# Reordering ScalarE's and VectorE's work in the attention head groups of a fused decoder block

## The reference, cut to what matters

```python
x = x + attn(layernorm(x))      # 16 heads of 32, ALiBi bias, 30*tanh(s/30), causal softmax
x = x + xattn(layernorm(x), memory, mask)     # one head, width 512, 128 memory rows
x = x + ffn(layernorm(x))       # silu(x @ q(gate_w) * sg) * (x @ q(up_w) * su) @ q(down_w) * sd
```

## Time and profile before

| | |
|---|---|
| time, median of 3 runs (lowest to highest) | 563.09 us (561.78 to 563.39) |
| time of the profiled execution | 563.1 us |
| its span, first to last instruction | 561.0 us |
| mean granted TensorE clock | 0.994 of full |
| TensorE busy | 547.0 us, 97% of the span |
| VectorE, ScalarE, GpSimd busy | 352.7, 268.0, 286.4 us |
| transposes of group 2 (head group 2 of g = 1) | begin at 114.06 us |
| `scores(2, 0)` | begins at 132.44 us |
| `scores` on TensorE | 1.4 us, `context` 1.9 us, a projection of 12 products 2.8 us |
| four transposes of one tile on TensorE | 0.37 us from one tile to the next |
| `normalize_context` on VectorE | 2.6 us (112.41 to 115.05) |
| GpSimd rounds a slab behind `low_part` of head group 2 | 117.37 to 120.23, 193.02 to 195.67, 260.61 to 263.26 |
| attention ends, feed-forward begins | about 262.7 us |

### The profile page before, as it was taken

One profiled execution on the slowest core, in us unless ns is written; L12 is line 12 of the kernel. 1 busy time (PEld: TensorE's weight loads), 2 busy tenths in 40 slices (PEclk: granted clock), 3 DMA queues, 4 the chain that ended last, 5 costly groups with the idle time before them and its releaser, 6 DMA issues.

```text
span 561.0 us, 10139 instructions
## 1 busy us (share of the span) xinstructions
PE 547.0 (97%) x3946; PEld 428.9 (76%) x3946; DVE 352.7 (63%) x701; ACT 268.0 (48%) x485; POOL 286.4 (51%) x258
## 2 busy tenths in 40 slices
PE   8999999989989999999999999999999999999997
PEld 7787888768868888888888888766686667866675
DVE  7997877895676667578787885345633564244422
ACT  6747976856845687567744352033401333023310
POOL 4297798965494554996794336324400343013320
PEclk9999999989989999999999999999999999999999
DMA  8951231452123520129571902200001000100001
GB/s 295 339 212 39 78 96 56 150 190 77 39 77 94 171 56 3 58 69 285 204 270 55 302 3 92 77 0 1 1 37 39 0 1 0 58 19 1 0 20 56
DMA packets 43422, 50.74 MB, mean 90 GB/s; under 512 B 2544, under 2 KB 25072, under 8 KB 43376
## 3 DMA queue, kind: packets, MB, share of 16 engines
q1 hardware_dynamic: 43376, 50.10, 27.2%
HBM read 36.46 MB, written 13.63 MB: 89 GB/s over the span
## 4 chain that ended last, share of the span: by engine, by line
PE 83%; POOL 7%; DVE 5%; ACT 2%; issue 2%; DMA 1%; DVEq 0%; ACTq 0%; POOLq 0%
PE bank L287 34%; PE bank L433 23%; PE bank L453 16%; PE bank L282 2%; PE bank L375 2%; PE bank L360 2%; POOL x_res L735 2%; PE bank L385 2%; POOL q_w L721 2%; POOL q_w L719 2%; POOL probs L712 1%; DVE q_m L1200 1%; PE bank L352 1%; POOL reduced L704 1%; ACT kT L856 1%
## 5 line engine op out<-in xcount | busy, mean ns | idle before, releaser
L287 PE MATMUL bank<-reduced 128*128 128x512 f32 x936 | 226.0, 398 | 3.5 <-DVE x_res L1167 2.6
L287 PEld LDWEIGHTS bank<-reduced 128*128 128x128 f32 x936 | 175.2, 190 | 42.2 <-issue 4.9
L814 POOL TENSOR_TENSOR f_parts<-fused,f_parts 128x512 fp32r<-128x512 f32 x48 | 62.9, 1310 | 159.3 <-ACT f_parts L1047 159.3
L1029 ACT ACTIVATE tanh_g<-bank,half_gate 128x512 f32<-128x512 f32 x48 | 33.0, 688 | 150.8 <-PE bank L433 139.2
L453 PE MATMUL bank<-reduced,f_parts 128*128 128x512 f32 x384 | 88.4, 390 | 0.0
L453 PEld LDWEIGHTS bank<-reduced,f_parts 128*128 128x128 f32 x384 | 71.8, 188 | 15.0
L1361 DVE SCALAR_TENSOR_TENSOR silu<-tanh_g,bank 128x512 f32<-128x512 f32 x48 | 32.9, 685 | 64.0 <-ACT tanh_g L1029 63.9
L433 PE MATMUL bank<-reduced 128*128 128x512 f32 x288 | 72.0, 402 | 0.0
L433 PEld LDWEIGHTS bank<-reduced 128*128 128x128 f32 x288 | 54.1, 188 | 12.9
L712 POOL TENSOR_SCALAR_AFFINE_SELECT probs<-probs 128x1024 f32<-128x1024 f32 x32 | 36.9, 1160 | 44.9 <-ACT probs L881 44.9
L719 POOL TENSOR_TENSOR q_w<-q_w,q_m 128x512 f32<-128x512 f32 x36 | 49.3, 1370 | 10.2 <-DVE q_m L1202 10.2
(11 more groups left out here) (123 smaller groups left out, 725.8 us busy)
## 6 DMA issues: line engine op xcount, KB each, us to landing
quantized<-q_w SPq DMA_DIRECT2D x36, 256.0 KB, 3.3
reduced<-quantized SPq DMA_DIRECT2D x12, 512.0 KB, 7.0
memT_sb<-in_memT SPq DMA_DIRECT2D x16, 256.0 KB, 5.0
mem_sb<-in_mem SPq DMA_DIRECT2D x16, 256.0 KB, 5.6
out<-y_sb SPq DMA_DIRECT2D x16, 256.0 KB, 2.0
q_w<-in_gate_w SPq DMA_DIRECT2D x12, 256.0 KB, 3.1
q_w<-in_up_w SPq DMA_DIRECT2D x12, 256.0 KB, 3.2
x_res<-in_x SPq DMA_DIRECT2D x3, 1024.0 KB, 9.3
```

Source lines behind the costliest of these rows:

```text
L287: ins = pe.matmul(dst, stationary, moving, start=(n == 0), stop=(n == len(pairs) - 1))
L814: pool.tensor_tensor(f_lo[:, f, :], fused[:, f % 2, :], f_hi[:, f, :].bitcast(F32), ALU.subtract).then_inc(f_lo_ready, 1)
L1029: act.activation(tanh_g[:, f % 2, :], src[:], ACT.Tanh, scale=half_gate[:, f:f + 1]).then_inc(tanh_ready, 1)
```

## The change

No instruction is added or removed. The order in three queues and two bank numbers change:

- TensorE: `turn_x(g + 1, 2)` writes the bank of Q and `turn_x(g + 1, 3)` that of K; before it was the other way round.
- ScalarE, head group 0 of g = 2 and 3: the second exponential of the probabilities is taken ahead of `cross_second(g - 2, 3)` and `cross_first(g - 2, 4)`.
- ScalarE, head group 2: Q is copied out ahead of K, and the high part of the context is made between the second and third turned tile, not ahead of all four.
- VectorE, head group 1, g of 1 and more: the third tile of the output projection is added ahead of the third slab's preparation.
- VectorE, head group 2, g of 1 and more: of the four normalized tiles for cross attention only the first is made ahead of the low parts of the turned tiles, three behind them.
- VectorE, head group 3: of the next group's statistics one tile stands ahead of cross attention's step 1 and three, with the moments, behind it.

```diff
@@ TensorE, head group 2
                 for i in range(GT):
-                    turn_x(g + 1, i, (S_BANK, S_BANK + 1, K_BANK, Q_BANK)[i])
+                    turn_x(g + 1, i, (S_BANK, S_BANK + 1, Q_BANK, K_BANK)[i])
@@ ScalarE, head group 0
                     k_out(g, 1)
-                    cross(g - 2, 3)
+                    cross_first(g - 2, 3)
+                    exp(g, 0, 2)
+                    cross_second(g - 2, 3)
                     cross_first(g - 2, 4)
-                    exp(g, 0, 2)
@@ ScalarE, head group 2
+                q_out(g, 3)
                 k_out(g, 3)
-                q_out(g, 3)
-                context_high(g, 1)
-                for i in range(GT):
+                for i in range(GT):
+                    if i == 2:
+                        context_high(g, 1)
                     x_high(g + 1, i)
@@ VectorE, statistics
-            def next_stats(g):
-                if g < G:
+            def next_stats(g, tiles=range(GT)):
+                if 0 in tiles and g < G:
                     dve.wait_ge(x_group_loaded[g], 16)
-                for i in range(GT):
+                for i in tiles:
                     norm_stats(0, g, i, token_tile(g % G, i))
-                norm_moments(0, g)
+                if GT - 1 in tiles:
+                    norm_moments(0, g)
@@ VectorE, head group 1
                     wo_out(g - 1, 1)
+                    wo_out(g - 1, 2)
                     prepare_slabs(slabs[2:3])
-                    wo_out(g - 1, 2)
                     wo_out(g - 1, 3)
@@ VectorE, head group 2
                 if g:
-                    norm_apply(1, g - 1, g - 1)
+                    norm_apply(1, g - 1, g - 1, range(1))
                 prepare_slabs(slabs_at(PREPARED, g, 2))
...
                 for i in range(GT):
                     x_low(g + 1, i)
+                if g:
+                    norm_apply(1, g - 1, g - 1, range(1, GT))
@@ VectorE, head group 3
                 if g < G - 1:
-                    next_stats(g + 2)
+                    next_stats(g + 2, range(1))
                     if g:
                         cross(g - 1, 1)
+                    next_stats(g + 2, range(1, GT))
                 if g:
                     prepare_slabs(slabs[1:])
```

## The result

The changed kernel takes 558.74 us in the median of 6 runs (556.93 to 560.32), the kernel before 563.13 us beside it (561.78 to 564.58): a ratio of 0.9921, 95% interval 0.9898 to 0.9944. It is faster, by 4.4 us. The forecast of 556.0 us was 2.7 us too low; the range of 553.0 to 560.0 held it, the forecast's own range of 554.3 to 557.4 did not. In the changed kernel, lines behind L965 are one to six numbers higher: L1101 is L1103, L1107 is L1109, L1128 is L1130, L1167 is L1169, L1200 and L1202 are L1202 and L1204. In experiments 4 and 5 they are L1102, L1108, L1129, L1168, L1201 and L1203.

The account below looks back on a forecast made before the run. TensorE bounds the kernel, busy 547.0 of 561.0 us. Gains 1.5 (transposes) + 4.4 (group 1) + 2.9 (group 2) = 8.8, less 1.7 of new stops: 563.1 - 7.1 = 556.0 us; own range 554.3 to 557.4, full range 553.0 to 560.0.

Parts of the forecast that it names:

- Banks, Q ahead of K: TensorE's transposes: 0.5 us of idle time goes in each of groups 0, 2 and 3, together 1.5 us.
- Group 0's share: Group 0's transposes: 0.5 us of TensorE idle time gained by the bank swap and Q copied first.
- Group 1: Group 1, head group 2: context from 115.5, scores at 117.5 instead of 120.41; 2.9 us plus 1.5 us half clock, 4.4 us.
- Rival B: Group 1: VectorE's backlog keeps a stop of 1 us or more and the half clock; 558.5, up to 559.5 us; chance 0.12.
- Exponential in group 2: Group 2's projections: GpSimd's chain 1.4 us earlier, stop 2.6 to 1.2 us, half clock's 1.5 us gone; 2.9 us.
- Rival A: Group 2: a 1.2 us rest lowers the clock too; 557.5 us, 558.9 if the exponential gives nothing; chance 0.17.
- The three late tiles: VectorE behind the low parts: tiles take 2.9 us; new stops 0.4 (group 1), 0.3 (group 2), 1.0 behind the attention; 1.7 us.
- The step from tiles to `fuse(0, 0)`: Behind the attention: tiles push context, two slabs and `fuse(0, 0)`; reciprocal from 271.74 to about 273.5, stop 1.0 us (0 to 2.5).
- Rival C: Behind the attention: all three tiles blocked, 4.7 us, long stop and half clock; 559.3 us, to 562.6 with group 1; chance 0.07.
- Rival D: Groups 1, 2 and 3: late tiles cost more than they free, 3 x 3.6 = 10.8 us, 566.8 us; chance 0.04.

Follow-up runs that it names:

- experiment 4: The changed kernel with only the exponential of head group 0 back at its old place, behind `cross_first(g - 2, 4)`: 562.01 us, ratio 0.9981.
- experiment 5: The kernel before with only the two bank numbers, Q copied out ahead of K, and `context_high` between the turned tiles: 560.21 us, ratio 0.9946.
- experiment 8: The kernel of experiment 2 with the third output tile behind the third slab again, as before the change: 554.35 us, ratio 0.9857.
- experiment 2: The changed kernel with all four normalized tiles ahead of the low parts again in group 3 only: 554.33 us, ratio 0.9848.
- Experiment 6: The kernel of experiment 2 with the four normalized tiles ahead of the low parts in groups 1 and 2 too: 558.55 us, ratio 0.9903.
- experiment 3: The changed kernel with ten added dummy products of the identity inside TensorE's stop at L401 in group 3: 557.32 us, ratio 0.9886.
- experiment 9: The kernel of experiment 2 with VectorE's cross attention step 6 ahead of the last slab of head group 0: 553.11 us, ratio 0.9813.
- experiment 10: The kernel of experiment 9 with the exponential of head group 0 back at its old place: 553.27 us, ratio 0.9838.
- experiment 1: The changed kernel timed again with no edit: 558.63 us, ratio 0.9924.

## Why the prediction came out as it did

**Banks, Q ahead of K: right.** The idle time of the earlier trace rows is gone in every group (1.8 us in the four groups together before, where the forecast had 2.0 us at stake). Group 0's share cannot be seen in the profile after, whose start is 0.5 us slower, but can be in experiment 8, whose context of head group 1 begins at 104.25; before, it began at 104.66. The part is worth more alone (2.7 us) than the 1.5 us of the forecast, because the stop in group 1 shrinks as well.

**Group 1: right to 0.1 us, in part by luck.** Context at 115.50 (forecast 115.5) behind the masks, scores at 117.38 (117.5), clock 1.00. The third output tile was rightly put down as absorbed by the masks. That the times agree so closely is luck: the forecast's times leave out group 0's 0.5 us, and the profiled execution started about as much late. In experiment 2, without the late start, context begins at 115.12 and scores at 117.01. Experiment 6 prices the split at 4.2 us there (forecast for the group 4.4). Rival B falls.

**Exponential in group 2: right.** The stop is 1.13 us (1.2), the clock stays, experiment 4 gives 3.4 us (2.9). The chain is the forecast's too: GpSimd's L704 begins at 143.50, 5.9 us earlier than before, and TensorE's wish for the bank 4.4 us earlier (155.9 against 160.34), so 1.5 us are gained (1.4). Rival A falls: 1.13 us of rest did not lower the clock.

**The three late tiles: the step that was mis-sized.** The tiles themselves were sized well: 2.75 us in group 1 and 2.84 us in group 3 (forecast 2.9), and the new stops of 0.4 and 0.3 us in groups 1 and 2 did not come. (The lower end of the forecast's 125.2 to 127.4 for VectorE at group 1's cross attention is not the sum of its terms, which is 124.5; VectorE was there at 125.4 and waited 0.44 us for the product.) Behind the attention the forecast was a stop of 1.0 us and no half clock, with the reciprocal of `normalize_context(3, 3)` delayed by 2.3 us against TensorE's course. Measured was a stop of 2.27 us and a delay of 4.4 us: TensorE's last context comes 8.4 us earlier than before (262.20 against 270.59), the reciprocal only 4.0 us (267.72 against 271.74). The step from tiles to `fuse(0, 0)` kept the old price of the two slabs, about 2.5 us (they take 263.59 - 259.10 = 4.5 us in the profile after, and 258.51 - 256.00 = 2.5 us in experiment 2). Tiles pushed the slabs under GpSimd's instructions, and the collision that was priced for the tiles was not priced for what they push. This is 2.0 us of the delay, and the stop is one of those behind which the clock fell. In the median that is 1.3 us more (experiment 3).

In all, this place costs 4.3 us (experiment 2) where the forecast had 1.0 us. Of these 3.3 us, 0.7 us are made up by the two stops that did not come; the 2.6 us left are the 2.7 us by which the forecast was too low. That the time lies in the range is luck in this respect: its upper part was there for rivals A and B, which did not come. Rival C had the outcome and the place, a long stop and its half clock behind the attention, 559.3 us by the prediction and 558.7 us measured, with a chance of 0.07. Its cause did not come true: it had all three tiles blocked, 4.7 us, and they took 2.84 us. Rival D's size, 10.8 us in three places, falls by the profile after: in groups 1 and 2 the late tiles make no stop. Its direction was nearer than its chance of 0.04 says: the tiles free 4.2 us in group 1 and cost 4.3 us in group 3.

The rule of the Trainium skill ("SBUF — State Buffer", section "Who interferes with whom") on VectorE and GpSimd excluding each other is borne out: the same L1202 takes 1.51 us in the profile after and 0.41 us in experiment 2, and L1109 stays at 0.62 us from one to the next in both, with GpSimd's L704 beside it. It should have been applied to every `tensor_scalar` behind the moved one.

## What to carry to other kernels

When an instruction is moved to later in a queue, price again everything behind it that can collide with another engine, not the moved instruction alone. A split that pays where the queue is in arrears can cost where it is not: look at the idle time ahead of the wait in each iteration, and split only there. Look for the instruction that stands wrongly ahead of an urgent one in its own queue (experiment 9), before speeding up the chain that feeds it (experiment 10).

## What the runs showed of the hardware

Behind one and the same stop, whether the clock falls and for how long differs between executions. Of the 23 runs of the kernel before beside experiments 1, 2, 4 and 5, the fastest took 559.92 us and the slowest 565.04 us, with mean granted clocks of 0.998 and 0.989, while every kernel with no stop above 1.5 us behind the kernel's start had all its runs within 0.2 to 1.1 us, at clocks of 0.998 and more. After the same 2.3 us stop at L401 the clock was at 0.50 for 6.5 us in one execution and for about 3.5 us in another (experiment 1), and the fastest run of the same kernel had a mean clock of 0.999. After the 2.6 us stop at group 2's projections it was at 0.50 in the profile before and stayed at 1.00 in that of experiment 5, where it fell behind a stop of 1.8 us instead. So a stop of 1.8 to 2.8 us cost its length plus between nothing and 2.9 us; the largest was seen in the profiled execution of the changed kernel, and that single profile would have made the change look 1.6 us worse than its median, by its long half clock and its late start together.
